# Moving the feed-forward, router and transpose results of an eight-sublayer transformer kernel to other PSUM banks

## The reference, cut to what matters

```python
x = x + jnp.tanh(g_xattn[0]) * _L0_xattn_ref(_layernorm(x), ctx, ctx, pos, mask_ik0, Wq, Wk, Wv, Wo)   # 32 heads of 128, rope
x = x + jnp.tanh(g_ffn[0]) * _L0_ffn_ref(_layernorm(x), base_W, gate_W, lora_A, lora_B)                # dense + top 2 of 28 LoRAs
x = x + jnp.tanh(g_xattn[1]) * _L1_xattn_ref(_layernorm(x), ctx, mask_ff0, ...)                        # 32 heads of 128, RMS norm
x = x + jnp.tanh(g_ffn[1]) * _L1_ffn_ref(_layernorm(x), qweight, scales, zeros, bias)                  # quantised dense
x = x + jnp.tanh(g_xattn[2]) * _L2_xattn_ref(_layernorm(x), ctx, ctx, ...)                             # 32 heads of 16
x = x + jnp.tanh(g_ffn[2]) * _L2_ffn_ref(_layernorm(x), ...)                                           # shared + top 2 of 16 experts
x = x + jnp.tanh(g_xattn[3]) * _L3_xattn_ref(_layernorm(x), ctx, mask_ff0, ...)                        # 32 heads of 128, RMS norm
x = x + jnp.tanh(g_ffn[3]) * _L3_ffn_ref(_layernorm(x), gate_w, gate_b, expert_w, expert_b)            # top 1 of 8 experts
```

```python
def _L0_ffn_ref(x, base_W, gate_W, lora_A, lora_B):
    base = xf @ base_W.T
    top_vals, top_idx = jax.lax.top_k(xf @ gate_W.T, 2)
    top_probs = softmax(top_vals); gate_full = scatter(top_probs, top_idx)
    h = jnp.einsum('nd,erd->ner', xf, lora_A) * (gate_full * 2.0)[:, :, None]
    return base + jnp.einsum('ner,eor->no', h, lora_B)

def _L3_ffn_ref(x, gate_w, gate_b, expert_w, expert_b):
    gates = softmax(xf @ gate_w.T + gate_b); selected = argmax(gates)
    return sum over j of where(selected == j, xf @ expert_w[j].T + expert_b[j], 0)
```

## Time and profile before

| | |
|---|---|
| median of 3 runs | 2846.93 us (2845.59 to 2851.8) |
| profiled execution, its own time | 2845.59 us |
| its span in the profile | 2843.8 us |
| granted TensorE clock, mean | 0.947 |
| busy share of the span: PE, DVE, ACT, POOL | 88%, 65%, 46%, 45% |

### The profile page before, as it was taken

The page is one execution under the profiler, slowest core; times in us unless marked ns, Lnnn a source line. Parts: engine busy times, 40 slices in busy tenths (PEclk is TensorE's granted clock), DMA queues, the critical chain, the costliest instruction groups (busy, mean ns, idle before and its releaser), DMA issues. The chain is left out here.

```text
span 2843.8 us, 42469 instructions
## 1 busy us (share of the span) xinstructions
PE 2510.0 (88%) x13827; PEld 2126.2 (75%) x13827; DVE 1859.0 (65%) x3455; ACT 1303.1 (46%) x3752; POOL 1283.2 (45%) x1423
## 2 busy tenths in 40 slices
PE   3899999997899999998988886878589999999865
PEld 2788888886678888887767775755468888888643
DVE  3677777767677777777747664532467777776765
ACT  2445454553245555555435443123145555555323
POOL 4545455453134444444336554334344444444345
PEclk9899999998899999999999997899799999999878
DMA  3111111111012222212000002169211111110047
GB/s 111 46 37 34 38 35 38 30 35 38 11 32 101 93 94 78 80 37 68 30 8 5 8 8 67 40 236 314 73 34 48 34 38 37 35 31 12 8 169 245
DMA packets 69102, 178.95 MB, mean 63 GB/s; under 512 B 10515, under 2 KB 11217, under 8 KB 66682
## 3 DMA queue, kind: packets, MB, share of 16 engines
q1 hardware_dynamic: 52048, 112.25, 12.3%
q0 software_dynamic: 13632, 61.10, 6.5%
q10 hardware_dynamic: 3210, 2.89, 0.3%
HBM read 157.84 MB, written 37.25 MB: 69 GB/s over the span
## 5 line engine op out<-in xcount | busy, mean ns | idle before, releaser
L1169 ACT ACTIVATE W<-S,nmx 128x128 f32<-128x128 f32 x768 | 297.6, 394 | 47.6 <-DVE nmx L1457 47.6
L1933 POOL TENSOR_SCALAR rn<-ss 128x5 f32<-128x5 f32 x128 | 25.5, 199 | 628.5 <-DVE ss L1400 628.5
L1066 ACT ACTIVATE sq<-B_qkv 128x640 f32<-128x640 f32 x128 | 90.3, 706 | 427.1 <-PE B_qkv L664 427.1
L1954 POOL TENSOR_TENSOR S<-S,mask 128x512 f32<-128x512 f32 x192 | 251.1, 1308 | 17.8 <-ACT S L1013 17.6
L1475 DVE SCALAR_TENSOR_TENSOR X<-B_out,gates,X 128x512 f32<-128x512 f32 x200 | 150.1, 751 | 164.2 <-PE B_out L664 162.8
L1993 POOL TENSOR_TENSOR W<-W,rden 128x512 f32<-128x512 f32 x192 | 200.3, 1043 | 104.7 <-DVE rden L1462 104.7
L715 PE MATMUL B_s<-kT,qT_h 128*128 128x256 f32 x768 | 207.7, 347 | 39.3 <-DVE xnT_l L1311 39.3
L664 PE MATMUL B_out<-ring_h,oT_h 128*128 128x512 f32 x516 | 208.4, 404 | 14.3 <-DVE kT L1447 10.8
L664 PE MATMUL B_qkv<-ring_h,xnT_h 128*128 128x512 f32 x512 | 216.0, 422 | 5.0 <-DVE xnT_l L1311 5.0
L664 PE MATMUL B_out<-ring_l,oT_h 128*128 128x512 f32 x516 | 207.4, 402 | 1.0 <-issue 1.0
L664 PE MATMUL B_out<-ring_h,oT_l 128*128 128x512 f32 x516 | 207.0, 401 | 0.8 <-issue 0.8
(11 more groups left out here) (452 smaller groups left out, 8179.9 us busy)
## 6 DMA issues: line engine op xcount, KB each, us to landing
raw<-in_pieces SPq DMA_DIRECT2D x270, 256.0 KB
slots_y<-S SPq DMA_DIRECT2D x31, 256.0 KB
slots_y<-y SPq DMA_DIRECT2D x15, 256.0 KB, 7.0
X<-in_x ACTq DMA_DIRECT2D x8, 256.0 KB, 2.6
raw<-in_ctxT SPq DMA_DIRECT2D x8, 256.0 KB
rows_x<-xn SPq DMA_DIRECT2D x8, 256.0 KB, 2.0
out_x<-X SPq DMA_DIRECT2D x8, 256.0 KB, 3.3
raw<-in_quant SPq DMA_DIRECT2D x4, 256.0 KB
```

The lines of the kernel that those rows point to most:

```text
L1066: act.activation(sq[:, :], B_qkv[:, 0:HG + P], ACT.Square).then_inc(*squared.now((layer, u)))
L1169: t = act.activation(W[:, k, cols(r)], S[:, k, cols(r)], ACT.Exp, bias=nmx[:, k, r:r + 1], accum_out=den[:, k, r:r + 1])
L1954: pool.tensor_tensor(S3, S3, m.unsqueeze(1).to_broadcast([P, R, P]), ALU.add).then_inc(*masked.now((layer, u)))
```

## The change

Only bank names change, in the writers and their readers. No instruction is added, taken away or moved. By the borders at which each stands:

- `ln_turn` of every norm that is not of the third attention or the third feed-forward: from `B_kT` (attention) or `B_sc` (feed-forward) to `B_pt`
- `low` from `B_pt` to `B_sc`; `turn_low` from `B_qT` to `B_oT`; `ffn0` and `ffn1` from `B_oT` to `B_out`
- `route3` from `B_qT` to `B_sc`; `rank3` from `B_qkv` to `B_sc`

```diff
         def turn_bank(stage, b):
 
-            if (stage, b) in plan.between:
-                return B_qT, "qT"
-            return (B_kT, "kT") if stage in ("attn0", "attn1", "attn3") else (B_sc, "sc")
+            return (B_qT, "qT") if (stage, b) in plan.between else (B_pt[:, :], "pt")
 
         def router_bank(stage):
-            return (B_kT, "kT") if stage == "ffn2" else (B_qT, "qT")
+            return (B_kT, "kT") if stage == "ffn2" else (B_sc, "sc")
...
                 hg = piece(plan.weights0[0])
-                bank_free("pt")
-                products(B_pt[:, 0:HL + E0], [(xn_cols(c, b), tuple(m[:, cols(c, HL + E0)] for m in hg)) for c in range(CH)]
+                bank_free("sc")
+                products(B_sc[:, 0:HL + E0], [(xn_cols(c, b), tuple(m[:, cols(c, HL + E0)] for m in hg)) for c in range(CH)]
                          ).then_inc(*low_done.now(b))
-                read["pt"] = low_read.of(b)
+                read["sc"] = low_read.of(b)
...
-                bank_free("qT")
+                bank_free("oT")
                 for k in range(2):
-                    t = pe.transpose(B_qT[0:HH, cols(k)], hs[:, b % 2, cols(k, HH)], ident[:, :])
+                    t = pe.transpose(B_oT[0:HH, cols(k)], hs[:, b % 2, cols(k, HH)], ident[:, :])
                 t.then_inc(*low_turned.now(b))
-                read["qT"] = hsT_lo.of(b)
+                read["oT"] = hsT_lo.of(b)
...
-                bank_free("oT")
+                bank_free("out")
                 pairs = [(xn_cols(c, b), two(w0, w1, c)) for c in range(CH)]
                 pairs += [(tuple(m[:, cols(k)] for m in hsT), tuple(m[0:HH, cols(k, D)] for m in lb)) for k in range(2)]
-                products(B_oT[:, :], pairs).then_inc(*ffn0_done.now(b))
-                read["oT"] = x_add.of(("ffn0", b))
+                products(B_out[:, :], pairs).then_inc(*ffn0_done.now(b))
+                read["out"] = x_add.of(("ffn0", b))
...
                     router("ffn3", b, E2, E3)
-                    read["qT"] = logits_read.of(b)
+                    read["sc"] = logits_read.of(b)
...
-                bank_free("qkv")
-                pe.matmul(B_qkv[:, 0:E3], before, onehot3[:, b, :], start=True, stop=False)
-                pe.matmul(B_qkv[:, 0:E3], ones, count3[:, b, :], start=False, stop=True).then_inc(*ranked.now(b))
-                read["qkv"] = slot_made.of(("read", b))
+                bank_free("sc")
+                pe.matmul(B_sc[:, 0:E3], before, onehot3[:, b, :], start=True, stop=False)
+                pe.matmul(B_sc[:, 0:E3], ones, count3[:, b, :], start=False, stop=True).then_inc(*ranked.now(b))
+                read["sc"] = slot_made.of(("read", b))
```

More of the change, by code:

```diff
@@ L849, in ffn1 @@
                     pe.wait_ge(*pick_made.of(0))
-                bank_free("oT")
-                products(B_oT[:, :], [(xn_cols(c, b), two(w0, w1, c)) for c in range(CH)], [(pick1, bias[:, :])]
+                bank_free("out")
+                products(B_out[:, :], [(xn_cols(c, b), two(w0, w1, c)) for c in range(CH)], [(pick1, bias[:, :])]
                          ).then_inc(*ffn1_done.now(b))
-                read["oT"] = x_add.of(("ffn1", b))
+                read["out"] = x_add.of(("ffn1", b))
             def router(stage, b, first_col, n):
@@ L1192, in low @@
                         act.wait_ge(*low_turned.of(b - 2))
-                    copy(hs[:, b % 2, :], B_pt[:, 0:HL]).then_inc(*low_copied.now(b))
+                    copy(hs[:, b % 2, :], B_sc[:, 0:HL]).then_inc(*low_copied.now(b))
                 if part == 5:
@@ L1201, in turn_low @@
                     act.wait_ge(sem, value)
-                copy(hsT[0], B_qT[0:HH, 0:2 * P]).then_inc(*hsT_hi.now(b))
+                copy(hsT[0], B_oT[0:HH, 0:2 * P]).then_inc(*hsT_hi.now(b))
                 spare_reader[:] = [ffn0_done.of(b)]
@@ L1549, in low @@
                     then()
-                    dve.tensor_copy(rt[:, 0, :], B_pt[:, HL:HL + E0]).then_inc(*low_read.now(b))
+                    dve.tensor_copy(rt[:, 0, :], B_sc[:, HL:HL + E0]).then_inc(*low_read.now(b))
                 if part == 1:
@@ L1585, in turn_low @@
                 dve.wait_ge(*hsT_hi.of(b))
-                sub(hsT[1], B_qT[0:HH, 0:2 * P], f32(hsT[0])).then_inc(*hsT_lo.now(b))
+                sub(hsT[1], B_oT[0:HH, 0:2 * P], f32(hsT[0])).then_inc(*hsT_lo.now(b))
             def ffn0(b):
                 dve.wait_ge(*ffn0_done.of(b))
-                add_to_x(b, B_oT, gates[:, 4:5], ("ffn0", b))
+                add_to_x(b, B_out, gates[:, 4:5], ("ffn0", b))
             def fill_pick():
@@ L1599, in ffn1 @@
                 dve.wait_ge(*ffn1_done.of(b))
-                add_to_x(b, B_oT, gates[:, 5:6], ("ffn1", b))
+                add_to_x(b, B_out, gates[:, 5:6], ("ffn1", b))
             def softmax(stage, b, dst, src, n):
@@ L1773, in route3 @@
                     then()
-                    dve.tensor_tensor(rt[:, 4, 0:E3], B_qT[:, 0:E3], gate_b[:, :], ALU.add).then_inc(*logits_read.now(b))
+                    dve.tensor_tensor(rt[:, 4, 0:E3], B_sc[:, 0:E3], gate_b[:, :], ALU.add).then_inc(*logits_read.now(b))
                     dve.wait_ge(*logits_read.of(b))
@@ L1809, in slots3 @@
                     dve.wait_ge(*slot_made.of(("sum", b - 1)))
-                dve.tensor_tensor(work3[:, 0, :], B_qkv[:, 0:E3], region3, ALU.add).then_inc(*slot_made.now(("read", b)))
+                dve.tensor_tensor(work3[:, 0, :], B_sc[:, 0:E3], region3, ALU.add).then_inc(*slot_made.now(("read", b)))
                 dve.wait_ge(*slot_made.of(("read", b)))
```

## The result

| | before | after |
| --- | --- | --- |
| median of the timed runs | 2846.26 us | 2921.1 us |
| lowest, highest | 2845.47, 2851.8 us | 2916.92, 2924.77 us |
| profiled execution | 2845.59 us | 2910.31 us |
| its span, mean granted TensorE clock | 2843.8 us, 0.947 | 2908.5 us, 0.940 |

The ratio is 1.0259 with a 95% interval of 1.024 to 1.0277, so the change costs 74.8 us by the medians. The forecast was 2913 us, in a range of 2868 to 2945 us. The two profiled executions differ by 64.7 us where the terms sum to 67. The profiled execution of the changed kernel was the fastest of its five; the four others had a granted clock of 0.936 to 0.938.

The account below looks back on a forecast made before the run. TensorE, busy for 88% of the span, was taken as the bound, with only idle time at layer borders to move. 0.5 + 32 + 9.5 + 25 = 67 us on 2845.6 gave 2913 us, range 2868 to 2945 us.

Parts of the forecast that it names:

- Edit 1: Norms turned into `B_pt`: the scores' 39.3 us wait moves to `turn_p`; +0.5 us, between -4 and +4.
- Edit 2: First border, `ffn0` into `B_out`: it waits for the low part of k; 32 us for this border.
- The term of the stalls: Steps 69 to 73: `ffn0` starts only after the low part of k (L1447), 26.7 us in all.
- the norms' term: Steps 69 to 71: two norms share a bank, VectorE idles 1.45 us in each step, 4.4 us together.
- the clock's term: First border: matmuls after longer stalls at half clock, 4 us for five blocks; 14 us by the skill's rule.
- the 3 us that the exponentials should give back: First border, three steps: the scores' exponentials on ScalarE are done under the stall, 1 us off each.
- The early steps: Steps 64 to 68: `ffn0` loses its `oT_l` waits, `low` starts 4.8 us later; 0, between -5 and +5.
- Edit 3: Second border, `ffn1` into `B_out`: waits in steps 131 and 132, clock 2 us; 9.5 us, between 5 and 13.
- Edit 4: Last layer's router and ranks into `B_sc`: waits 12.9 and 8 us, clock 4; 25 us, between 13 and 32.
- Absorbed: Rival: VectorE's chain moves forward and partly absorbs the stalls; +31 us, 2877 us; chance 0.2.
- The clock makes it dearer: Rival: all long stalls drop the clock; +95 us, 2940 us; chance 0.12.
- Faster: Rival: the scores' 39.3 us of waits go without coming back at `turn_p`; 2837 us; chance 0.04.

Follow-up runs that it names:

- experiment 1: The kernel before with only the products of the first feed-forward (`ffn0`) put into `B_out`: 2869.6 us against 2844.11, ratio 1.0073.
- experiment 3: The kernel before with only the norms turned into `B_pt`: 2864.09 us, ratio 1.0064.
- experiments 6 to 8: Kernel before with feed-forward products in `B_out` only where no `turn_q` stands ahead; norms in `B_qT`, `turn_low` in `B_kT`; both: 2838.2, 2838.01, 2831.15 us.

## Why the prediction was right

**Edit 1** was right in kind: the wait went one piece forward, 39.3 us to 37.6 us. At the two starts the change gained 0.5 and 1.6 us where I had put a loss of 0.5 in all; inside its bounds, and of the 1.6 us kernels without this edit show up to 1.2.

**Edit 2** was forecast at 32 us and measured 35.9. The term of the stalls, 26.7 us, was read as what `ffn0` loses beyond its old start, so the waits that it had before (2.09 and 0.52 us) have to come off. In experiment 1, the edit alone, the five waits for L1447 are 6.38, 6.22, 5.14, 8.05 and 3.53 us, 26.7 us more than before, and each block is within 0.4 us of its term. In the change they sum to 27.6 us, 24.9 more than before; the blocks of steps 72 and 73 are 1.7 us under their terms.

From the addition before step 69 to the one of `ffn0` in step 73, at 738.78 and 820.06 us of the trace before, the change loses 33.8 us: these 24.9, 4.6 us of other idle time on TensorE, and 4.3 us of longer matmul time. The 4.6 us stand against the norms' term of 4.4: they are waits for `xnT_l` and `qk`, and one of 2.65 us of `times_v` for `spare_l`, which `turn_low` now puts through `B_oT` and which had been put at under 1 us. The second norm's 1.45 us is the idle time of VectorE to the digit; in experiment 3 the same stretch loses 4.7 us. The 4.3 us stand against the clock's term of 4; 1.8 of them are in the five blocks of `ffn0`, from its first product to the next piece (28.8 us after and 27.0 before), and in experiment 1 these blocks took 32.0 us, +5.0.

One term was wrong: the 3 us that the exponentials should give back did not appear. They stand on ScalarE behind the copies of the projection, which wait for TensorE, and so are not done under the stall; in step 70 `W<-S` starts at 791.15 us and is still the piece right ahead of the copy of `hs` at 792.69. The early steps, taken as even, lost 1.7 us, and they were not even in themselves. TensorE's timeline, after (compare):

```profile
682.22 0.55 PE L662 MATMUL B_s<-ring_h,xnT_h 128*128 128x252 f32 x1 [8.17 <-DVE S L1452]
...
701.25 0.35 PE L662 MATMUL B_s<-ring_h,xnT_h 128*128 128x252 f32 x1 [2.86 <-DVE S L1452]
```

`low` of batch 1 started 4.8 us late, exactly as the bound said, and most of it was given back where `ffn0` no longer waited for `oT_l`: experiment 1 gains 2.6 us there.

**Edit 3** was forecast at 9.5 us (its terms make 9.3) and measured 9.2 in the change and 7.5 by itself.

**Edit 4** was forecast at 25 us and measured 24.7, with some luck: the waits came out smaller than their terms and the clock dearer. Waits were put at 12.9 and 8 us, and TensorE's idle time grew by 16.9 us; the clock was put at 4 us, and the busy time of the same matmuls grew by 7.8 us. Router and ranks alone cost 19.1 us (10.7 us idle, 8.4 us matmul time), the norms alone 12.4 us (3.2 and 9.3); the two add up to more than the change because the matmul time is paid once. I had given the clock to the router alone, and put the norms' cost down as a wait. The two waits that I had said would exceed 20 us are 16.7 us.

**The sum** of 67 us stands against 64.7 us between the profiled executions, and 74.8 between the medians. The 10 us are the difference between the changed kernel's profiled execution and its median. A lower granted clock goes with it in the four timed runs (0.936 to 0.938 against 0.940); the trace of one execution can't say more, and this part is open.

**The rivals.** "Absorbed" falls with the 27.6 us: VectorE's chain did not move forward. "The clock makes it dearer" wanted some 14 us of clock at the first border and falls with 4.3 us in steps 69 to 73; that is one execution, and what the clock has in the 10 us of the medians is open. By the rule of the Trainium skill that I cited (TensorE: Matmul & The Clock Gate, HAM oscillation) it should have been up to 14 us; four of the five blocks do begin at half clock, 0.63 us a matmul, but parts of them ran so before, and the block of step 73 keeps 0.40 us after 1.76 us of idle time. "Faster" fell in experiment 3. The rule that independent groups should rotate through banks (Perfetto Trace Analysis, Matmuls, in the Trainium skill) agrees with experiments 6 to 8, which gain 6 to 13 us, but does not choose among the banks: the change follows it at the scores too, and loses. Here what counts is when the bank's last reader comes in the queue.

## What to carry to other kernels

A wait in the list is worth what is left when the next piece in the same queue has had to wait for the same event: here 39.3 us in the list were worth nothing in one bank and some 8 us in another. When a piece gets another bank, look up the last reader of that bank, its place in its engine's order, and what stands ahead of it; the difference of the two start times, block by block, is the price, and with the edit alone it came out at 26.7 us, as read. Idle time and matmul time have to be priced apart: at the last router the waits of two edits added up, while the cost of the lower clock was paid once.

## What the runs showed of the hardware that was not expected

An idle time of about 3 us does not always end in half-clock matmuls. TensorE's timeline in the kernel before, and after it that of the kernel after, each from the first product behind such a wait:

```profile
1328.10 0.47 PE L664 MATMUL B_out<-ring_h,oT_h 128*128 128x512 f32 x1 [3.68 <-DVE kT L1447]
1328.41 0.39 PE L664 MATMUL B_out<-ring_l,oT_h 128*128 128x512 f32 x1
...
1328.88 0.39 PE L664 MATMUL B_out<-ring_h,oT_h 128*128 128x512 f32 x1
```

```profile
1363.13 0.47 PE L662 MATMUL B_out<-ring_h,oT_h 128*128 128x512 f32 x1 [2.84 <-DVE kT L1445]
1363.44 0.39 PE L662 MATMUL B_out<-ring_l,oT_h 128*128 128x512 f32 x1
...
1363.89 0.45 PE L662 MATMUL B_out<-ring_h,oT_h 128*128 128x512 f32 x1
1364.14 0.63 PE L662 MATMUL B_out<-ring_l,oT_h 128*128 128x512 f32 x1
```

After 3.68 us of idle time the products took 0.39 us behind the first one, at a granted clock of 1.00 (the level of 2.4 GHz) to the end of the piece. After 2.84 us they began at 0.39 us too and fell to 0.63 us a microsecond later, where the granted clock is 0.50 (1.2 GHz). Ahead of either wait TensorE had done the same transposes and the same projection, 4.9 us without a gap. So the length of one wait does not tell the clock behind it, and a price per stall read off one block does not carry to the next.
